# A fused transformer block on one core: half of the restacking DMAs moves from SyncE's queue to ScalarE's

## The reference, cut to what matters

```python
h = onehot(x) @ embeddings                      # x: (8, 256) ids, h: (8, 256, 256)
q, k, v = heads(layernorm(h) @ w_qkv)           # 16 heads of 16
q, k = rotary(q), rotary(k)
h = h + merge(softmax(q @ k.T / 4) @ v) @ w_proj
y = layernorm(h)
chosen = argmax(y @ gate_w.T)                   # one of 8 experts for each token
h = h + y + (y @ expert_w[chosen].T)
```

## Time and profile before

| | |
|---|---|
| median of 3 runs | 338.32 us (337.97 to 338.34) |
| the profiled execution | 337.72 us |
| its span in the trace | 335.9 us |
| busy: PE, DVE, ACT, POOL | 83%, 73%, 35%, 25% of the span |
| length of a step once the pipeline is full | 33.47 us |

### The profile page before, as it was taken

How to read it: one execution, slowest core, us unless ns; L and a number is a source line. 1 busy time by engine, 2 the same in 40 slices (tenths; PEclk the granted TensorE clock), 3 DMA queues, 4 the chain that set the end, 5 groups by cost and what they waited for, 6 DMA issues and landing times.

```text
span 335.9 us, 5461 instructions
## 1 busy us (share of the span) xinstructions
PE 280.2 (83%) x2000; PEld 200.0 (60%) x2000; DVE 244.5 (73%) x595; ACT 118.4 (35%) x245; POOL 84.7 (25%) x96
## 2 busy tenths in 40 slices
PE   0457281877698899999999899989999999999894
PEld 0345170555465577766776677667766766667673
DVE  8353254678769887988798879887988885657763
ACT  3012131246354544434443444344434453441000
POOL 5235248472201310222032303220210121120211
PEclk9995755589979999999999999999999999999999
DMA  3619699009809608800790079008900000000000
GB/s 112 254 45 129 71 104 104 0 11 119 83 3 125 68 0 101 92 4 31 99 93 5 31 101 93 2 31 101 94 28 8 0 4 33 2 1 33 0 31 31
DMA packets 16197, 19.13 MB, mean 57 GB/s; under 512 B 2524, under 2 KB 13607, under 8 KB 16044
## 3 DMA queue, kind: packets, MB, share of 16 engines
q1 hardware_dynamic: 15404, 18.25, 38.6%
q0 software_dynamic: 768, 0.55, 1.3%
HBM read 5.30 MB, written 2.10 MB: 22 GB/s over the span
## 4 chain that ended last, share of the span: by engine, by line
PE 41%; DVE 23%; issue 11%; POOL 9%; DMA 7%; SPq 4%; ACT 3%; POOLq 0%; DVEq 0%; ACTq 0%
PE e_bank L419 13%; PE f_bank L419 7%; PE o_bank L536 6%; DVE acc L885 5%; DVE neg_max L806 4%; POOL qk L345 3%; PE t_pair L501 3%; DMA stacks<-parts 3%; DMA stacks<-max_rows 3%; SPq L284 3%; PE s_pair L419 2%; POOL h L332 2%; PE m_bank L548 2%; PE m_bank L419 2%; POOL res L363 1%
## 5 line engine op out<-in xcount | busy, mean ns | idle before, releaser
L687 ACT ACTIVATE probs<-t_pair 128x512 f32<-128x512 f32 x128 | 69.7, 597 | 91.4 <-PE t_pair L501 90.9
L806 DVE TENSOR_REDUCE neg_max<-s_pair 128x2 f32<-128x512 f32 x120 | 76.7, 681 | 14.0 <-PE s_pair L473 14.0
L419 PE MATMUL e_bank<-ew_h,y_h 128*128 128x512 f32 x92 | 40.4, 439 | 4.6 <-DVE acc L881 2.7
L501 PE MATMUL t_pair<-stacks 50*128 50x256 f32 x192 | 35.1, 310 | 3.9 <-DMA stacks<-max_rows 1.9
L885 DVE SCALAR_TENSOR_TENSOR acc<-e_bank,mask,acc 128x256 f32<-128x256 f32 x66 | 28.8, 477 | 11.3 <-PE e_bank L419 10.9
L501 PEld LDWEIGHTS t_pair<-stacks 50*128 50x128 f32 x192 | 24.4, 186 | 20.7 <-issue 17.1
L419 PE MATMUL e_bank<-ew_h,y_l 128*128 128x512 f32 x92 | 36.3, 395 | 0.0
L419 PE MATMUL e_bank<-ew_l,y_h 128*128 128x512 f32 x92 | 36.3, 395 | 0.0
L536 PE MATMUL o_bank<-probs,vals 128*32 128x256 f32 x512 | 35.1, 393 | 1.3 <-ACT max_rows L662 1.3
L473 PE MATMUL s_pair<-stacks 48*128 48x256 f32 x176 | 35.1, 325 | 0.4 <-DVE neg_max L806 0.4
L345 POOL TENSOR_TENSOR qk<-rope_a,rope_b 128x512 f32<-128x512 f32 x16 | 20.7, 1292 | 54.8 <-DVE rope_b L793 54.8
(11 more groups left out here) (123 smaller groups left out, 557.0 us busy)
## 6 DMA issues: line engine op xcount, KB each, us to landing
stacks<-parts SPq DMA_DIRECT2D x48, 128.0 KB
stacks<-parts SPq DMA_DIRECT2D x12, 256.0 KB
ew_raw<-in_expert_w SPq DMA_DIRECT2D x1, 2048.0 KB, 7.9
late_stacks<-parts SPq DMA_DIRECT2D x16, 128.0 KB
out<-res SPq DMA_DIRECT2D x8, 256.0 KB, 2.1
late_stacks<-parts SPq DMA_DIRECT2D x4, 256.0 KB
probs<-in_w_qkv SPq DMA_DIRECT2D x2, 384.0 KB, 3.4
stacks<-max_rows SPq DMA_DIRECT2D x24, 8.0 KB
```

Of the source, the lines that this page charges most:

```text
L419: m = mm(o, a(c), w(c), start=(n == 0), stop=(n == 3 * C - 1))
L501: m = mm(t_pair[:, half, c * N:(c + 1) * N], stacks[b % STACKS][r:r + KM, pair, 1, c * P:(c + 1) * P], stacks[b % STACKS][r:r + KM, pair, ...
L687: nc.scalar.activation(probs[:, (2 * v + half) % RING, :, :].rearrange("p c n -> p (c n)"), t_pair[:, half, :], ACT.Exp, scale=SCALE).then ...
L806: v.tensor_reduce(neg_max[:, k // 4, :, 4 * half + k % 4], score_pair(b, k)[:, half, :].rearrange("p (t n) -> p t n", t=NT), AX.X, ALU.max ...
```

## The change

`restack` is cut in two. `restack_first` stays with SyncE in its old place and issues the five DMAs of half 0. `restack_second` issues the five of half 1 from ScalarE's stream, directly behind `values(k)`. It has the same waits (`qkl_ok`, `t_ps`, and for batch 2, whose stack shares memory with the raw expert weights, `ew_l_ok`). Sizes, sources, targets and semaphore stay.

```diff
-            def restack(b):
+            def restack_first(b):
                 wait(sp, qkl_ok, b * NT + NT)
                 wait(sp, t_ps, (b - STACKS) * NH + NH)
-                for half in range(2):
-                    r = 64 * half
-                    ...
+                r = 0
+                both = stacks[b % STACKS][r:r + HD, :, :, :].bitcast(F32)
+                sp.dma_start(both.rearrange("d j k n -> d j (k n)"),
+                             parts[:, 0, Q_HIGH:K_HIGH + 1, :].bitcast(F32)).then_inc(stack_in, 16)
+                for i, (q_part, k_part) in enumerate(((Q_LOW, K_HIGH), (Q_HIGH, K_LOW))):
+                    for k, part in enumerate((q_part, k_part)):
+                        at = r + (i + 1) * HD
+                        sp.dma_start(stacks[b % STACKS][at:at + HD, :, k, :].bitcast(F32),
+                                     parts[:, 0, part, :].bitcast(F32)).then_inc(stack_in, 16)
...
+            def restack_second(b):
+                wait(act, qkl_ok, b * NT + NT)
+                wait(act, t_ps, (b - STACKS) * NH + NH)
+                if b == 2:
+                    act.wait_ge(ew_l_ok, 8)
+                r = 64
+                both = stacks[b % STACKS][r:r + HD, :, :, :].bitcast(F32)
+                act.dma_start(both.rearrange("d j k n -> d j (k n)"),
+                             parts[:, 1, Q_HIGH:K_HIGH + 1, :].bitcast(F32)).then_inc(stack_in, 16)
+                for i, (q_part, k_part) in enumerate(((Q_LOW, K_HIGH), (Q_HIGH, K_LOW))):
+                    for k, part in enumerate((q_part, k_part)):
+                        at = r + (i + 1) * HD
+                        act.dma_start(stacks[b % STACKS][at:at + HD, :, k, :].bitcast(F32),
+                                     parts[:, 1, part, :].bitcast(F32)).then_inc(stack_in, 16)
...
                     for k in batches(front, "v", g_at):
                         values(k)
+                        restack_second(k)
```

More of the change, by code:

```diff
@@ L297, in step @@
                 if here(b, 2):
-                    restack(b + 2)
+                    restack_first(b + 2)
                 if here(b, 1):
```

## The result

The changed kernel takes 355.06 us (median of four, 354.66 to 355.7) against 338.33 us (337.97 to 338.55) in the same comparison: a ratio of 1.0481, interval 1.0446 to 1.0517, 16.7 us more. The forecast was 351.5 us with a range of 343.5 to 358. The sign was right, and so was the main mechanism, the held stream of ScalarE. The terms of the clock and of the late start behind batches 2 and 3 were too small, that of the full pipeline too large, and for the low clock behind batch 2 the cause that the forecast gave is not shown.

What follows compares the result with a forecast made beforehand. A gapless chain through TensorE and VectorE, closely awaiting ScalarE's results, was taken as the bound; 3.2 + 0.9 + 2.25 + 4.4 + 2.6 = 13.3 us on 337.72 gave 351.1, stated as 351.5 us, range 343.5 to 358.

Steps and rivals of the forecast that it cites:

- held stream: ScalarE behind each copy of v: five issues keep it from copies and exponentials for 3.2 us.
- The issue's price: ScalarE behind each copy of v: 0.64 us an issue, 3.2 us for five, with no copies or exponentials meanwhile.
- What is removed, and the second queue: SyncE issues five DMAs fewer per batch; transfers stay at 118 GB/s, limited by the DMA engines: gain 0.
- Batch 0: Start of the kernel: later copies are covered by the wait for the DMAs of `parts`, with 0.8 us to spare: cost 0.
- Batch 1: Behind its v: copies to `ew_h` start late, and GpSimd's gapless chain passes on the whole delay: +3.2 us.
- Batch 2: Behind its v: TensorE's visit 2.7 us late, the 1.85 us wait at the maxima gone: +0.9 us, clock separate.
- the meeting: Rival: ScalarE's and SyncE's issues hinder each other in batches 2 and 3, 5.2 us more, 356.7 us; chance 0.25 with related cases.
- Batch 3: Behind its v: first exponential, TensorE's visit and VectorE's `o_l` late by 2.25 us: +2.25 us, clock separate.
- Batches 4 to 7: Full pipeline: late exponentials and `o_l` carry 1.1 us a step to TensorE, four steps: +4.4 us.
- The clock's trigger: TensorE's clock falls behind the new holes of batches 2 and 3, 1.3 us each, +2.6 us; 0 in the full pipeline.
- shorter: Rival: ScalarE's issues take 0.40 us, or more is covered, some 5 us cost, 343.5 us; chance 0.17 for 342 to 347.
- only hands over: Rival: an issue keeps ScalarE under 0.1 us, so not slower, 336.5 to 338.5 us; chance 0.06.

Runs made afterwards that it cites:

- e1: Kernel before, SyncE issuing all ten DMAs, plus six unread ScalarE copies behind each v: 354.91 us, ratio 1.0439.
- e2: Changed kernel with ScalarE's issues moved to idle places for batches 1 and 4 to 7, batches 2 and 3 back on SyncE: 338.31 us, ratio 0.9989.
- e12: Changed kernel, but for batches 2 and 3 SyncE issues its five DMAs only after ScalarE has issued its own: 352.5 us, ratio 1.0382.
- e6: Changed kernel with all ten DMAs of each restacking issued by ScalarE behind v, none by SyncE: 383.82 us, ratio 1.1322.
- e8: The change for batch 1 alone, SyncE issuing all ten for the other batches: 341.41 us, ratio 1.0093 to the kernel before.
- e5: Changed kernel with only one DMA (256 KB) on ScalarE behind each v and nine on SyncE: 338.54 us, ratio 1.0004.
- e10: Kernel before plus eight unread TensorE products in its 1.85 us wait at batch 2's maxima: 337.43 us, ratio 0.9946.
- e7: Changed kernel plus 12 unread TensorE products in each of the holes behind v of batches 2 and 3: 351.28 us, ratio 1.0362.
- e3: The change for batches 4 to 7 alone, SyncE issuing all ten for batches 0 to 3: 342.9 us, ratio 1.0117 to the kernel before.
- e4: Kernel before with SyncE's two DMAs of the ones for batch 2 issued behind that batch's restacking instead of ahead: 338.07 us, ratio 0.9961.
- e9: The change for batches 2 and 3 alone, SyncE issuing all ten for the others: 349.55 us, ratio 1.0272 to the kernel before.

## Why the prediction was right, step by step

**The issue's price**: taken as 0.64 us, five as 3.2. Measured 0.55 and four in 2.60 us. Right. The bound from below, a mere handing over, did not occur; e1 shows that a hold of that length by itself gives the loss. That ScalarE copies nothing in this time was wrong: its copies run beside the issues if they were handed over first (e2), and the first issue runs beside the copy of v. So at batch 1 the five issues delay what follows v by 2.7 us and not by 3.2.

**What is removed, and the second queue**: taken as 0 at an unchanged 118 GB/s. The time was right, since e2 gains nothing. The rate was not. Over the whole restacking of batches 2 and 3 (the stretch in which the DMA engines' share is above 0.6) the windows give 141 GB/s in 11.5 us and 131 in 11.8 us for the change, 125 in 12.75 us and 121 in 13.25 us before, and 124 in 13.0 us and 123 in 12.8 us for e12, where one queue issues after the other. So two queues issuing at once moved the same bytes about a tenth faster, which the prediction had named as a sign that it is wrong. The Trainium skill, "DMA: Bandwidth & Descriptors", section "Issuing engines are not separate DMA queues", holds for the time here and not fully for the rate. The faster of the two transfers belongs to the slower kernel, so it bought nothing.

**Batch 0**: 0. Right: v1 stands where it stands in kernels without them. With ten (e6) it comes 2 us late, held by TensorE's transposes, so the cover that I had named is real and short.

**Batch 1**: +3.2. The change shows 3.7, the part alone (e8) 3.2 by its ratio. The path was right. The amount came out partly by luck: the issues delay the chain by 2.7 us, and in the change another 1.0 us arises behind `xn`, where the clock was lower than before, a term that the forecast did not have here.

**Batch 2**: +0.9, and +1.3 for the clock, measured 5.1. This is the term of the sum that was mis-sized most. The wait at the maxima went, as said. But TensorE's visit was 3.2 us late (4.87 us behind v instead of 1.65), not 2.7, through the meeting, and the low clock lasted 13 us, where I had priced one group of 16 products and half as much again. The visit at 101.28 stands 21.2 us behind v, before 16.3: 4.9 = 3.2 for the late start - 1.85 for the wait that went + 3.5 that are left, over a stretch at 0.50. So the term of the clock was 3.5 instead of 1.3. It is a remainder of one execution, and kernels without the hole had a low clock there too (e5, e8, e10), so how much of it the issues bring is open.

**Batch 3**: +2.25 and +1.3, measured 4.8. The visit is 3.1 us late (5.30 us behind v instead of 2.16): 0.9 us above the forecast, through the meeting. The rest, 1.7 us, is the clock; e7 gives 1.9. The meeting alone makes the exponentials 0.9 us (batch 2) and 1.2 us (batch 3) later by e12; the 0.5 and 0.9 us above the forecast are what is left of that, because the issues start with the copy of v.

**Batches 4 to 7**: +4.4, measured 3.2 in the trace, and 4.0 by the ratio of e3. The term was too large by up to 1.2. Each step costs 0.88 to 0.97 us (1.0 in e3) instead of 1.1, because the issues start with the copy of v and not behind it. The last batch costs only 0.5, with no next v behind it. No fall of the clock, as taken.

**The clock's trigger**: right in place, since the clock fell behind both holes and not in the full pipeline. As a mechanism it is supported behind batch 3 by e7, and by e6, the only kernel of the study whose clock fell between 132 and 256 us, behind holes of 3.65 us that ten issues left (at 158 and 198 us). Behind batch 2 it is not: filling the hole only put the fall off (e7), the clock fell there without one (e5, e8, e10), and a wait of 1.57 us had a fall behind it in e4 and none in the change. What decides whether the clock falls, and how long it stays low, is open: 13 us behind a hole of 2.5 us, 7 behind one of 3.1, and 16 in e9.

**The rivals**: "shorter" and "only hands over" fall by the 0.65 us. The meeting holds in part (e12). The Trainium skill, "Perfetto Trace Analysis", section "DMA Instruction — HWDGE (DVE, Sync)", has the generator locked for one sequencer at a time; for ScalarE and SyncE the trace shows less than turns of whole issues, 4.8 us for ten where these would need 6.4. A lock over only some 0.48 us of each issue (an estimate, 4.8 / 10) would fit too; no run here tells whether it is a lock. The forecast left the meeting out of its sum. In the trace that sum fell short by 17.5 - 13.3 = 4.2 us: 1.4 for the late start through the meeting (0.5 and 0.9), 2.6 for the clock (2.2 and 0.4), 0.5 for batch 1 and 0.6 ahead of v1, less 1.2 for the full pipeline, 3.9 in all.

## What to carry to other kernels

An issue takes its engine's stream for 0.65 us. Where the engine has results behind it that others await, five issues cost what six copies that take as long cost, and the page's busy share does not show it: read what stands behind the place, not how idle the engine is. Issues belong behind the last awaited result of a slot, or on a queue that does nothing else. And a hole of TensorE can cost twice: the one of 3.1 us behind batch 3 cost itself and 1.9 us of low clock behind it. In parts of a kernel where the clock falls in some executions and not in others, one profile does not price that; compare medians, and look at the clock of several kernels at the same place.

## What the runs showed of the hardware

- An issue on ScalarE's queue does not wait for the copy ahead of it to end: it starts 0.01 to 0.06 us behind the copy's start, and in e2 five issues ran beside four copies. One issue behind a 0.6 us copy is thus free.
- SyncE and ScalarE issuing at once slow each other to 0.8 to 0.9 us an issue, ten in 4.8 us, between full turns (6.4 us) and no hindrance (3.2 us).
- With both issuing at once the restacking of batches 2 and 3 moved at 131 to 141 GB/s and took 11.5 to 11.8 us (the change); with one at a time it was 121 to 125 GB/s and 12.75 to 13.25 us (before, e12).
- TensorE's clock was still at 2.4 GHz through holes of 2.5 and 3.1 us and fell to 1.2 GHz after work had begun again, while in e9 it fell inside the hole (0.88 over 78 to 80 us). It then stayed there for 7 to 16 us. It also fell in the same part of the kernel behind idle times of 0.6 and 0.8 us (e5, 0.50 over 82 to 88 us), and stayed at 2.4 GHz behind one of 1.57 us (the change, 102.6 to 104.2 us), behind which it fell in e4.
